# Expert stage of a two-layer attention and feed-forward kernel: the lower f16 halves of the gathered rows turned by DMA from ACT's queue, and the split gate/up weights stored by expert

## The reference, cut to what matters

```python
x = hidden_states.reshape(-1, H)                      # 1600 tokens, H = 512
probs = softmax(x @ gate_weight.T); topv, topi = top_k(probs, 8)
active = scaled >= TAU                                # 0.05: small weights are dropped
...
def expert_step(acc, xs):                             # 32 experts
    w_gu, w_d, c_e = xs
    g, u = jnp.split(x @ w_gu.T, 2, axis=-1)          # 192 columns each
    h = jax.nn.silu(g) * u
    return acc + h @ w_d.T * c_e[:, None], None
```

## Time and profile before

| | us |
|---|---|
| median of 3 runs | 1823.49 |
| lowest, highest run | 1820.08, 1828.2 |
| the profiled execution, its own time | 1828.59 |
| span of the profile (first to last instruction) | 1826.8 |

### The profile page before, as it was taken

The page is one execution under the profiler, slowest core; times in us unless marked ns, Lnnn a source line. Parts: engine busy times, 40 slices in busy tenths (PEclk is TensorE's granted clock), DMA queues, the critical chain, the costliest instruction groups (busy, mean ns, idle before and its releaser), DMA issues. The chain is left out here.

```text
span 1826.8 us, 35630 instructions
## 1 busy us (share of the span) xinstructions
PE 1609.2 (88%) x11892; PEld 1000.0 (55%) x11911; DVE 1191.8 (65%) x2686; ACT 1035.6 (57%) x2563; POOL 612.5 (34%) x481
## 2 busy tenths in 40 slices
PE   4788999999999979989998787776489999999997
PEld 3655646646646545545555454554356666666664
DVE  4866796796796788786887677666833333333334
ACT  2447746746746637566665676653635555555554
POOL 4613303304304300000000122221157777777775
PEclk9788999999999989999999799876589999999999
DMA  8820120120120149786776200011446657665626
GB/s 270 284 92 10 50 81 10 51 80 10 53 79 10 59 132 346 241 294 199 233 249 218 92 2 29 29 37 55 126 92 142 165 134 171 142 139 140 155 47 217
DMA packets 145061, 226.58 MB, mean 124 GB/s; under 512 B 38049, under 2 KB 93601, under 8 KB 144760
## 3 DMA queue, kind: packets, MB, share of 16 engines
q1 hardware_dynamic: 108888, 195.90, 33.7%
q0 software_dynamic: 29344, 21.29, 7.1%
q10 hardware_dynamic: 6656, 7.11, 1.1%
HBM read 175.00 MB, written 98.80 MB: 150 GB/s over the span
## 5 line engine op out<-in xcount | busy, mean ns | idle before, releaser
L2760 PE MATMUL g_ps<-ring,xT 128*128 x1572 | 301.2, 327 | 0.7 <-issue 0.5
L1051 POOL TENSOR_TENSOR pr<-pr,sm 128x1444 f32<-128x1444 f32 (+1 forms) x64 | 137.2, 2143 | 384.9 <-DVE sm L1087 384.9
L2709 POOL DMA_INDIRECT acc<-rows,slot_sources x131 | 208.8, 1594 | 105.6 <-issue 56.5
L2866 DVE SCALAR_TENSOR_TENSOR hf<-sg,g_ps 128x192 f32<-128x192 f32 x131 | 46.4, 354 | 237.4 <-ACT sg L2815 237.4
L2760 PEld LDWEIGHTS g_ps<-ring,xT 128*128 128x128 f16 x1572 | 142.2, 98 | 72.6 <-issue 7.2
L2699 POOL DMA_INDIRECT xg<-xtab,slot_sources x131 | 138.1, 1054 | 81.9 <-issue 78.9
L2782 PE MATMUL d_ps<-ring,hT 128*128 x655 | 162.8, 379 | 0.7 <-ACT hT L2828 0.7
L1081 DVE TENSOR_REDUCE sm<-s_banks 128x2 f32<-128x722 f32 (+2 forms) x128 | 97.5, 762 | 68.8 <-PE s_banks L819 66.3
L973 ACT ACTIVATE pr<-s_banks,sm 128x361 f32<-128x361 f32 (+1 forms) x208 | 115.4, 563 | 32.9 <-DVE sm L1081 31.4
L876 PE MATMUL o_bank<-cT,N_hi 128*128 128x400 f16 x512 | 128.4, 332 | 1.8 <-ACT tern_a L626 0.6
L819 PE MATMUL s_banks<-kvp,qp 128*128 128x361 f16 (+1 forms) x624 | 119.3, 323 | 11.9 <-ACT pr L973 6.0
(11 more groups left out here) (326 smaller groups left out, 3847.6 us busy)
## 6 DMA issues: line engine op xcount, KB each, us to landing
split_f<-in_gu SPq DMA_DIRECT2D x64, 384.0 KB, 4.5
split_gu<-split_o SPq DMA_DIRECT2D x64, 384.0 KB, 3.1
ring<-split_gu SPq DMA_DIRECT2D x32, 768.0 KB
head<-in_head SPq DMA_DIRECT2D x16, 864.0 KB, 8.5
tern_w<-in_tern SPq DMA_DIRECT2D x48, 256.0 KB
split_f<-in_down SPq DMA_DIRECT2D x32, 384.0 KB, 4.1
split_d<-split_o SPq DMA_DIRECT2D x32, 384.0 KB, 3.7
ring<-split_d SPq DMA_DIRECT2D x32, 256.0 KB
```

What stands on the lines that cost most here:

```text
L1051: nc.gpsimd.tensor_tensor(pr[:, s % 3, 0:n], pr[:, s % 3, 0:n], small[:, s % 3, 2, 0:n].unsqueeze(2).to_broadcast([P, n, KEYS]), ALU.mult) ...
L2709: nc.gpsimd.indirect_dma_start(out=core.acc[i % NACC][:, :], out_offset=bass.IndirectOffsetOnAxis(ap=core.sources[:, i:i + 1], axis=0), in ...
L2760: last = nc.tensor.matmul(g_ps[i % 2][:, 0:2 * INTER], xT[:, i % 2, a * KT + k, :], ring(i, (2 * k + w) * 2 * INTER, 2 * INTER), start=((k ...
```

## The change

Three things change.

1. In `experts`, PE turns only the upper halves (4 transposes per tile, not 8). The lower half (128 x 512 f16) is turned by one DMA transpose per tile, SBUF to SBUF, issued from ACT: `turn_lo(i)`. Three are issued ahead, and `turn_lo(i + 3)` stands in ACT's loop turn i, where `copy_h(i - 1)` stood. `xT` gets NT = 4 places in place of 2. PE's `up(i)` and POOL's `gather` wait on a further semaphore each.
2. `copy_h` moves from ACT to DVE, between `copy_x(i + 1)` and `product(i)`; DVE's `copy_x` copies 512 columns, not 1024.
3. `split_gu` is laid out by expert: [pair, 2, partition, KT, 768]. Its store writes two runs of 1536 bytes per partition and block, not one of 3072, and the load of one expert reads one run of 6144 bytes per partition, not four of 1536.

```diff
@@ ExpertSplit.store
-            dst, out = self.core.split_gu[q][:, part], self.o[:, s, :]
+            dst = self.core.split_gu[q][:, :, part, :].rearrange("e p n -> p e n")
+            out = self.o[:, s, :].rearrange("p (e n) -> p e n", e=2)
@@ ExpertWeights.load
-        sp.dma_start(self.ring[:, r:d].rearrange("p (k n) -> p k n", k=KT),
-                     core.split_gu[q].rearrange("p k (e n) -> p k e n", e=2)[:, :, x, :]).then_inc(sem, 16)
+        sp.dma_start(self.ring[:, r:d], core.split_gu[q, x].rearrange("p k n -> p (k n)")).then_inc(sem, 16)
@@ experts: gather
-                        pool.wait_ge(x_turned.sem, x_turned.after(i - NX))
+                        o = i - NX
+                        pool.wait_ge(x_turned.sem, x_turned.after(o))
+                        pool.wait_ge(lo_turned[o % NT].sem, lo_turned[o % NT].after(o // NT))
@@ experts: turn_x on PE
-                    for k in range(2 * KT):
-                        last = nc.tensor.transpose(half(x_ps[i % 2], 2 * KT)[:, k, :], parts[:, k * P:(k + 1) * P],
+                    for k in range(KT):
+                        last = nc.tensor.transpose(half(x_ps[i % 2], KT)[:, k, :], parts[:, k * P:(k + 1) * P],
@@ experts: up on PE
+                        pe.wait_ge(lo_turned[i % NT].sem, lo_turned[i % NT].after(i // NT))
@@ experts: ACT
-                def copy_h(i):
-                    act.wait_ge(h_turned.sem, h_turned.after(i))
-                    if i >= 2:
-                        act.wait_ge(down.sem, down.after(i - 2))
-                    nc.scalar.activation(hT[:, i % 2], half(h_ps[i % 2], 3), ACT.Copy).then_inc(h_copied.sem, 1)
+                def turn_lo(i):
+                    act.wait_ge(x_in[i % NX].sem, x_in[i % NX].after(i // NX))
+                    if i >= NT:
+                        act.wait_ge(gu.sem, gu.after(i - NT))
+                    nc.scalar.dma_start_transpose(xT[:, i % NT, KT:2 * KT], xg[:, i % NX, DIM // 2:DIM].bitcast(F16)
+                                                  ).then_inc(lo_turned[i % NT].sem, 16)
...
+                for i in range(NT - 1):
+                    turn_lo(i)
                 for i in range(TILES + 2):
                     if i >= 2:
                         weigh(i - 2)
-                    if 1 <= i < TILES + 1:
-                        copy_h(i - 1)
+                    if i + NT - 1 < TILES:
+                        turn_lo(i + NT - 1)
@@ experts: DVE
-                for i in range(TILES):
+                for i in range(TILES + 1):
                     if i + 1 < TILES:
                         copy_x(i + 1)
-                    product(i)
-                    low(i)
+                    if i >= 1:
+                        copy_h(i - 1)
+                    if i < TILES:
+                        product(i)
+                        low(i)
```

More of the change, by code:

```diff
@@ L1308, in ffn0 @@
     d_turned, added = Steps(core, "down_turned"), Steps(core, "down_added", per=CB, depth=1)
-    core.split_gu = nc.dram_tensor("split_gu", [PAIRS, P, KT, 2 * 2 * 2 * INTER], F16, kind="Internal").ap()
+    core.split_gu = nc.dram_tensor("split_gu", [PAIRS, 2, P, KT, 2 * 2 * INTER], F16, kind="Internal").ap()
     core.split_d = nc.dram_tensor("split_d", [PAIRS, P, 2, 3 * DIM], F16, kind="Internal").ap()
@@ L2329 @@
 ROUND = 1.5 * 2.0 ** 23
-NX, NACC, NO = 8, 2, 6
+NX, NACC, NO, NT = 8, 2, 6, 4
 class ExpertWeights:
@@ L2634, in experts @@
     x_turned, x_copied = Steps(core, "x2_turned"), Steps(core, "x2_copied")
+    lo_turned = Slots(core, "x2_lo_turned", NT, per=16)
     gu, gated, made = Steps(core, "gu2_sum"), Steps(core, "silu2"), Steps(core, "h2")
@@ L2645, in experts @@
         xg = core.xg
-        xT = core.sb(ctx, "xT", [P, 2, 2 * KT, P], F16)
+        xT = core.sb(ctx, "xT", [P, NT, 2 * KT, P], F16)
         sg = core.sb(ctx, "sg2", [P, 2, INTER], F32)
@@ L2758, in up @@
                         pe.wait_ge(w_ready, place[i][1])
+                        pe.wait_ge(lo_turned[i % NT].sem, lo_turned[i % NT].after(i // NT))
                     for k, w, a in terms:
-                        last = nc.tensor.matmul(g_ps[i % 2][:, 0:2 * INTER], xT[:, i % 2, a * KT + k, :],
+                        last = nc.tensor.matmul(g_ps[i % 2][:, 0:2 * INTER], xT[:, i % NT, a * KT + k, :],
                                                 ring(i, (2 * k + w) * 2 * INTER, 2 * INTER),
@@ L2857, in copy_x, with copy_h @@
                     dve.wait_ge(x_turned.sem, x_turned.after(i))
+                    if i >= NT:
+                        dve.wait_ge(gu.sem, gu.after(i - NT))
+                    nc.vector.tensor_copy(xT[:, i % NT, 0:KT], half(x_ps[i % 2], KT)).then_inc(x_copied.sem, 1)
+                def copy_h(i):
+                    dve.wait_ge(h_turned.sem, h_turned.after(i))
                     if i >= 2:
-                        dve.wait_ge(gu.sem, gu.after(i - 2))
-                    nc.vector.tensor_copy(xT[:, i % 2], half(x_ps[i % 2], 2 * KT)).then_inc(x_copied.sem, 1)
+                        dve.wait_ge(down.sem, down.after(i - 2))
+                    nc.vector.tensor_copy(hT[:, i % 2], half(h_ps[i % 2], 3)).then_inc(h_copied.sem, 1)
                 def product(i):
```

## The result

The changed kernel takes 1845.27 us in the median of 5 runs (1832.82 to 1852.57) against 1823.49 before: a ratio of 1.0107, 95% interval 1.0073 to 1.0142. The forecast was 1800 us, faster than before; the change made the kernel slower. In two later calls the same kernel measured 1.0082 (1.0053 to 1.0112) and 1.0090 (1.0056 to 1.0124) of before. The profiled execution is the fastest of the five, 1832.82 us, so it shows the loss at its smallest. Its expert stage began ten us earlier than that of before (first gather at 1318.40, before at 1328.76; two other profiles of the same changed kernel have it at 1327.2 and 1328.1, so this start varies between executions).

What follows compares the result with a forecast made beforehand. PE was taken to bound the kernel. The terms, -29.5 + 0.8 + 4 + 1 = -23.7 us, took the profiled 1828.6 us to 1804.9; that execution being 5.1 above the median, the forecast was 1800 us, range 1793 to 1850.

Steps and rivals of the forecast that it cites:

- What bounds the kernel: Expert stage: PE is busy all the time, so a column less on PE is time gained if others fit the turn.
- PE's part: PE's turn per tile: four transposes fewer, 0.225 us over 131 tiles, -29.5 us; turn from 3.64 to 3.42 us.
- ACT's part: ACT's turn per tile: the transpose's issue holds ACT 1.0 us, covered up to 1.88 us; cost nothing.
- Rival C: ACT is held too long by the transpose's issue, slower than before from 2.1 us: 1850 to 1889 us; chance 12%.
- DVE's part and the end: DVE's turn grows from 1.41 to about 1.64 us, cost nothing; final adds wait for the last copy_h, 0.8 us.
- The start: Tile 0's gate/up matmuls also wait for a DMA transpose: 0.7 us less to 1.9 more, taken as 1 us.
- The transfer: Each DMA transpose takes 0.6 us of all engines, between 0.44 and 0.81; landing hidden within 9.5 us.
- rival D: DMA transposes form one stream, each longer than a tile: 1910 us, or 2030 by the skill's figure; chance 10%.
- Scatters and gathers: POOL in the expert stage: late scatters cost 0 to 8 us, taken as 4; gathers keep 3.7 us reserve, cost nothing.
- The layout: Weights in DRAM: a faster load is hidden, counted as nothing; the store costs 0 to 2 us, taken as 0.
- rival B: POOL or a late gather bounds part of the stage: 8 to 37 us given back, 1804 to 1833 us; chance 16%.
- The signs: Profile after: tiles 3.42 us apart (wrong from 3.6), DMA share 0.77 to 0.87, PE not waiting for hc, POOL sometimes idle.

## Why the prediction was wrong, point by point

- **What bounds the kernel:** right. PE alone did, and a PE column less is time gained when the transfer is absent.
- **PE's part, -29.5 us:** the turn of 3.42 us was met exactly, but not in the mean. The load of four tiles' addresses, hidden before, shows once per group: 3.50 us, 20 us gained. The term was over-sized by 10 us.
- **ACT's part, a hold of 1.0 us, cost nothing:** the hold is 1.21 us in the median, inside the bounds and under 1.88, with single ones up to 2.7. In the run without weights the holds are the same and PE waits for hc for 0.9 us in 430. In the changed kernel silu does wait, for the gather in front of the issue. Rival C was not what happened.
- **DVE's part and the end:** copying 512 columns took 418 ns and 384 took 358, where 490 and 430 were reckoned; cost nothing, right. The end: DVE's adds began 1.07 us after the last `low` began, 0.27 before, so 0.8, as forecast.
- **The start, 1 us:** from PE's first transposes to the first gate/up matmuls 3.1 us (1322.12 to 1325.26) against 2.4: 0.7.
- **The transfer, 0.6 us of the engines:** 0.92 measured, above even the upper bound of 0.81. Without the weights it is 0.76, inside the bounds. So the bounds held beside scatters and gathers alone; beside the weights too, the packets last longer. The Trainium skill, "DMA: Bandwidth & Descriptors", section "Latency and other measured facts", has 261 GB/s for a transpose by DMA with a non-contiguous middle dimension, by which 0.131 MB would be an estimated 0.50 us; the traces say 0.92 and, without the weights, 0.76. The Trainium skill's figure of 1309 ns per block ("VectorE: DVE Perf Modes", section "The three transpose paths"), weighed in the prediction as rival D, did not come true as a serial price either: at the start of the stage, before any scatter, the first four blocks were issued and used within 3.2 us (1322.09 to 1325.26), and without weights a turning came every 3.52 us.
- **Scatters and gathers, 4 us:** this is the step that failed. The mechanism was named, in the prediction's own words that two turnings fall into a scatter's time and that a late gather stands ahead of silu, and it was priced at 1 us per load of weights. It took a scatter's worst landing to be 6.7 + 1.6 = 8.3 us; landings of 10.68 us occur. It called the gather's 3.7 us of reserve enough; a gather landing 6.35 us after its issue in place of 3.85, behind a POOL that is itself late by up to 5.3, is over it. The 9.5 us of cover of a turning held in the changed kernel, where PE waited for no turned half in the steady stage; they were exceeded, by turnings of 10.8 to 13.7 us, once the gathers came earlier. In place of 4 us the turning cost 35 to 39 (0.989 to 1.008 and more). I had added up the engines' time as a mean share, 0.77 to 0.87; the weights come in bursts during which the other transfers land late, and the run with spread loads, the same bytes at 0.9951, shows that this is most of it.
- **The layout, nothing:** right alone, at 0.9998. Beside turnings a cost of some 0.3% is not excluded.
- **The rivals:** the outcome is rival B by its mechanism, at the top of its 8 to 37 us given back: 35 to 39 came, with a gain of 20 in place of 29.5 to pay them from. So 1845.27 lies outside its 1804 to 1833. It had been given 16%, of which only 3 for a slower kernel. That the wide range to 1850 holds the measured time is luck: its upper end came from rival C, which did not happen.
- **The signs:** of those that were to prove the forecast wrong, PE waiting for hc and tiles 3.6 us or more apart (3.75) came true. The DMA share is 0.93 and not 0.77 to 0.87, and one turning in the chain landed after 9.99 us and not under 9.

## What to carry to other kernels

Work moved from a full engine to the DMA queues is to be priced against the bursts that they already carry, and not only against their mean share: set the worst landing seen beside the cover of every transfer that someone waits for, and ask what two of them in a row do. A transfer that nobody waits for (here weights that come three experts ahead) can be spread out at no cost (0.9997 in the kernel before), and that may be what pays for the move. An engine's in-order queue with an issue in front of its critical step hands each late arrival on; the one reordering tried here, 1.0331, made others wait longer.

## What was not expected of the hardware

A transpose by DMA of 128 x 512 f16 is 544 packets, holds ACTq for 1.21 us (up to 2.7) and takes 0.76 us of all 16 engines without the weight loads, 0.92 beside them. The DMA share says little of the room that is left: it reads 1.07 in a window where PE idles for 1 us and 0.91 in one where it idles for 8.4. What the packets of a burst do to those of another queue inside the engines was not measured; that the landings are late is shown, the arbitration behind it is not. Times of the changed kernel also spread more (1829.8 to 1852.6 us in 18 runs) than those of before (1820.1 to 1831.9, one far outlier aside). Why is not known.
